# LayerNorm statistics without the square root on ScalarE, issued two tiles ahead, in a fused attention and spiking feed-forward kernel

## The chip, the cores and the metric

The kernel runs on the 8 cores of one Trainium2 chip. Each core takes one batch element (4096 tokens of 1024 channels) and runs the same program; nothing passes between the cores. The metric is the device time of the slowest core, in microseconds, for one execution.

## What is computed

```python
xn = layernorm(x)                     # (x - mean) / sqrt(var + 1e-5), per token, C = 1024
# attention in windows: qkv = xn @ w_qkv; windows of 4 tokens, every 2 tokens, 8 heads
dots = einsum('bnqhd,bnkhd->bnhqk', q, k) * scale
o = einsum('bnhqk,bnkhd->bnqhd', softmax(dots), v)
s = scatter_add(o @ w_out + b_out)    # every token lies in two windows
# feed-forward with a spiking neuron of 5 steps
h = square(relu(xn @ W_fc.T));  y = h @ W_proj.T
g = silu(sum_over_5_steps(spike) / 5)
out = x + s * g
```

The five steps of the neuron depend on `y` alone and are computed as five thresholds on it.

## The kernel before

The program has two phases. Phase A (up to about 1336 us) does the LayerNorm, the projections and the windowed attention, and leaves xn transposed and the attention result `st` in DRAM. Phase C does the feed-forward on blocks of 256 tokens and writes the output. The change touches phase A only.

Phase A works on tiles of 128 tokens (32 of them) in groups of four; the loop over `i` (0 to 9) has four steps `j` each, so a step is numbered k = 4i + j. In step k three things are interleaved, each for another part of the sequence:

- LayerNorm of tile `tln` = k (for i up to 7): `ln_load` brings x into one of two `xt` buffers (the buffer is tln % 2), `ln_stats` computes mean and 1/sqrt, `ln_apply` writes the normalised tile in bf16 to one of two `xnb` buffers, `xn_transpose` turns it with eight TensorE transposes into a `pp` bank and copies it to `xnT` (on VectorE for even tiles, on ScalarE for odd ones).
- Projection of the group before (for i from 1 to 8): each step has two chunks, `qk_super` (four heads, 32 matmuls and four evictions on ScalarE) in steps j = 0 and 1, `v_tile` (16 matmuls, two evictions) in steps j = 2 and 3. The banks `pp0` and `pp1` serve all chunks and transposes in turn.
- Attention of tile t = k - 8 (for i from 2): `scores(t, g)` for two halves g of the heads, `softmax_merge(t, g)` (four exponentials on ScalarE, L496 and L501, then two reduces, a reciprocal and eight small merges on VectorE), `wt_and_o(t - 1, g)`, and `st_tile(t - 1)`, the output projection of the tile before, whose result VectorE adds the bias to (L604, L606) and SP stores (`st_sc<-stt`).

Each engine has one queue that it works off in the order in which the code is written; nothing is reordered. In a step of before the code is in this order: `ln_apply(k)`, `ln_load(k + 2)`, `scores` and `softmax_merge` of g = 0, first chunk, `scores` and `softmax_merge` of g = 1, `wt_and_o`, second chunk, `st_tile`, `xn_transpose(k)`, `ln_stats(k + 1)`.

`Walk2.op` records the instructions and works out the semaphore waits from names of buffers; where a buffer's last user has no semaphore yet, it takes the last instruction recorded so far on that engine, so a wait can be for a later instruction than the one that used the buffer. The reads of `xt` are: a sum on VectorE (L316), then a sum of squares by a Square activation with an accumulator on ScalarE (L318), which waits for L316 since both write `astat`. From these VectorE makes mean, variance (L321 to L325), ScalarE takes the square root (L328), VectorE the reciprocal and the bias (L331, L333), and ScalarE applies them (L342).

At the start SP issues eleven small loads of constants (L276 to L281), all of which every engine's first instruction waits for, POOL's first load of `w_qkv` too.

Of the kernel before, what the change touches and what calls it, by code (L numbers as in the profile page):

```python
# [7 lines left out]
F32 = mybir.dt.float32  # L8
# [144 lines left out]
def build_program(L=4096):  # L153
# [23 lines left out]
    rfL = np.zeros((128, 1), np.float32); rfL[126:128] = -0.5  # L177
    zer_h = nc.inline_tensor(np.zeros((128, 1), np.float32), "c_zero")
    eps_h = nc.inline_tensor(np.full((128, 1), 1e-5, np.float32), "c_eps")
    rz0_h = nc.inline_tensor(rz0, "c_rz0")  # L180
    rzL_h = nc.inline_tensor(rzL, "c_rzL")
    rf0_h = nc.inline_tensor(rf0, "c_rf0")
# [4 lines left out]
    def sb(name, shape, dtype, off):  # L187
        A[name] = nc.alloc_sbuf_tensor_at(name, shape, dtype, offset=SB_BASE + off)
        return A[name]

    sb("eye", [128, 128], BF16, 0)
    sb("ones1", [1, 128], F32, 256)
    sb("mA", [128, 132], BF16, 768)
# [82 lines left out]
    for name, hdl in (("eye", eye_h), ("ones1", ones_h), ("mA", mA_h),  # L276
                      ("mB", mB_h), ("rz0", rz0_h), ("rzL", rzL_h),
                      ("rf0", rf0_h), ("rfL", rfL_h), ("zero", zer_h),
                      ("eps", eps_h)):
        dma("sp", A[name][:], hdl.ap(), "smc", (), ("consts", "bout"))  # L280
    dma("sp", A["bout"][:], bout_d, "smc", (), ("consts", "bout"))  # L281
    for _e in ENGS:
# [23 lines left out]
    def ln_load(t):  # L306
        p = t % 2
        dma("sp", A["xt"][:, C * p: C * (p + 1)], x_d[128 * t:128 * (t + 1), :],
            "sx" + str(p), (), (f"xt{p}",), ckpt=True)

    def ln_stats(t):
        p = t % 2
        xt = A["xt"][:, C * p: C * (p + 1)]
        xn = A["xnb"][:, C * p: C * (p + 1)]
        st = A["astat"][:, 8 * p: 8 * p + 8]
        w.op("ve", lambda E, o=st, i=xt: E.tensor_reduce(o[:, 0:1], i, AX.X, ALU.add),  # L316
             reads=(f"xt{p}",), writes=(f"astat{p}",))
        w.op("ae", lambda E, i=xt, s=st, d=xn: E.activation(d, i, AF.Square,  # L318
                                                            accum_out=s[:, 1:2]),
             reads=(f"xt{p}",), writes=(f"astat{p}", f"xnb{p}"))  # L320
        w.op("ve", lambda E, s=st: E.tensor_scalar(s[:, 2:3], s[:, 0:1], inv_c, None, ALU.mult),  # L321
             reads=(f"astat{p}",), writes=(f"astat{p}",))
        w.op("ve", lambda E, s=st: E.tensor_tensor(s[:, 3:4], s[:, 2:3], s[:, 2:3], ALU.mult),
             reads=(f"astat{p}",), writes=(f"astat{p}",))
        w.op("ve", lambda E, s=st: E.scalar_tensor_tensor(  # L325
            s[:, 4:5], s[:, 1:2], inv_c, s[:, 3:4], ALU.mult, ALU.subtract),
             reads=(f"astat{p}",), writes=(f"astat{p}",))
        w.op("ae", lambda E, s=st: E.activation(s[:, 5:6], s[:, 4:5], AF.Sqrt,  # L328
                                                bias=A["eps"][:, 0:1]),
             reads=(f"astat{p}", "consts"), writes=(f"astat{p}",))  # L330
        w.op("ve", lambda E, s=st: E.reciprocal(s[:, 6:7], s[:, 5:6]),  # L331
             reads=(f"astat{p}",), writes=(f"astat{p}",))
        w.op("ve", lambda E, s=st: E.scalar_tensor_tensor(  # L333
            s[:, 7:8], s[:, 2:3], -1.0, s[:, 6:7], ALU.mult, ALU.mult),
             reads=(f"astat{p}",), writes=(f"astat{p}",))

    def ln_apply(t):
        p = t % 2
        xt = A["xt"][:, C * p: C * (p + 1)]
        xn = A["xnb"][:, C * p: C * (p + 1)]  # L340
        st = A["astat"][:, 8 * p: 8 * p + 8]
        w.op("ae", lambda E, i=xt, s=st, d=xn: E.activation(  # L342
            d, i, AF.Identity, scale=s[:, 6:7], bias=s[:, 7:8]),
             reads=(f"xt{p}", f"astat{p}"), writes=(f"xnb{p}",))
# [287 lines left out]
    for j in range(2):  # L632
        ln_load(j)
    ln_stats(0)
    for i in range(NS + 2):
        p, qcons = i - 1, i - 2
        if i == NS:
# [6 lines left out]
                  if 0 <= p < NS else [])  # L644
        for j in range(4):
            tln = 4 * i + j
            if i < NS:
                ln_apply(tln)
                if tln + 2 < NT:
                    ln_load(tln + 2)  # L650
            t = 4 * qcons + j
            if qcons >= 0:
                scores(t, 0)
                softmax_merge(t, 0)
            for ch in chunks[2 * j: 2 * j + 1]:
                (qk_super(*ch[1:]) if ch[0] == "qk" else v_tile(ch[1]))
            if qcons >= 0:
                scores(t, 1)
                softmax_merge(t, 1)
                if t >= 1:  # L660
                    wt_and_o(t - 1, 0)
                    wt_and_o(t - 1, 1)
            for ch in chunks[2 * j + 1: 2 * j + 2]:
                (qk_super(*ch[1:]) if ch[0] == "qk" else v_tile(ch[1]))
            if qcons >= 0 and t >= 1:
                st_tile(t - 1)
            if i < NS:
                xn_transpose(tln)
                if tln + 1 < NT:
                    ln_stats(tln + 1)  # L670
        if i >= 2 and (i - 2) % 2 == 0 and (i - 2) // 2 < 3:
            xnsc_block((i - 2) // 2)
        if i == NS:
# [170 lines left out]
```

How the kernel before makes its waits and increments, by code:

```python
        def body(E):  # L802
            watermark = {}
            for rec in w.prog[eng_name]:
                for s, v in sorted(rec["waits"].items()):
                    if v > 0 and watermark.get(s, -1) < v:
                        E.wait_ge(sems[s], v)
                        watermark[s] = v
                instr = rec["fn"](E)
                if rec["inc"] is not None:
                    instr = instr.then_inc(sems[rec["inc"][0]], rec["inc"][1])
                if rec.get("inc2") is not None:
                    instr.then_inc(sems[rec["inc2"][0]], rec["inc2"][1])
```

## Time and profile before

| what | us |
|---|---|
| median of the runs (2357.06 to 2360.82) | 2358.94 |
| the profiled execution | 2354.82 |
| span of its slowest core (core 0) | 2353.3 |
| spans of the other cores | 2342.7 to 2351.8 |

The profile is of core 0. The median of the runs is 4.1 us above the profiled execution. Over the span PE is busy 1706.7 us (73%), ScalarE (ACT) 764.5 us, VectorE (DVE) 721.1 us. In a timeline row the columns are start, duration, engine, line, operation, and in brackets how long the engine sat idle before it and what released it. SPq is the queue of SP, which issues DMAs.

### The profile page before, as it was taken

Reading aid. Unit: us, or ns where it says so; the run is one execution under the profiler, and the core shown is the slowest. Engines: PE = TensorE matmul, PEld = TensorE weight load, DVE = VectorE, ACT = ScalarE, POOL = GpSimd, SP = SyncE. Lnnn points to the kernel's source line nnn. Section 1 sums busy time; section 2 is a strip of 40 time slices with the busy share of each in tenths; the row PEclk is TensorE's granted clock in tenths of the full one; section 3 lists DMA queues with packets and bytes.
Section 4 is the critical chain, followed back from the end, with each engine's and each line's share of the span. In section 5 each row is a group of like instructions: output and inputs, shape, how many; then the busy total and the mean of one; then the engine's idle time right before and its main releaser. Section 6 shows DMA issues by size and latency. Waiting matters only on the chain.

```text
span 2353.3 us, 29180 instructions; the slowest of 8 cores (2342.7 to 2353.3 us)
## 1 busy us (share of the span) xinstructions
PE 1706.7 (73%) x10595; PEld 998.8 (42%) x10708; DVE 721.1 (31%) x1561; ACT 764.5 (32%) x1702; POOL 29.9 (1%) x60
## 2 busy tenths in 40 slices
PE   1366575666565665656675519999999999999997
PEld 0123232323233333323332206666666666666664
DVE  1013423333333324232334411222333333333222
ACT  2143323232323232322211004444444444444442
POOL 0000000000000000000000000000000000000000
PEclk9998687787777786876886659999999999999998
DMA  4510010030100200100205431111111111112110
GB/s 100 101 42 14 23 54 23 19 58 14 51 26 27 47 23 21 54 14 14 36 10 105 92 79 39 55 54 55 55 54 55 54 55 55 55 55 63 55 61 21
DMA packets 55585, 111.05 MB, mean 47 GB/s; under 512 B 7314, under 2 KB 23699, under 8 KB 54420
## 3 DMA queue, kind: packets, MB, share of 16 engines
q1 hardware_dynamic: 47380, 84.02, 10.8%
q0 software_dynamic: 8064, 25.17, 6.7%
q8 instruction: 87, 1.43, 0.3%
q14 instruction: 54, 0.44, 0.1%
HBM read 100.77 MB, written 33.55 MB: 57 GB/s over the span
## 4 chain that ended last, share of the span: by engine, by line
PE 50%; ACT 20%; DVE 13%; issue 11%; DMA 5%; DVEq 1%; ACTq 0%; another core or an unknown queue 0%; SPq 0%; POOLq 0%
PE pp L387 9%; PE psB L742 9%; PE psA L742 9%; ACT hrl L724 7%; PE pO L598 5%; PE pp L406 4%; ACT hsb L727 4%; PE pO L721 3%; DMA wq<-w_qkv 3%; PE pO L565 2%; PE pO L581 2%; DVE wb L527 2%; PE pp L721 2%; ACT expB L501 2%; DVE wb L523 2%
## 5 line engine op out<-in xcount | busy, mean ns | idle before, releaser
L387 PE MATMUL pp<-xnT,wq 128*128 128x512 bf16 (+1 forms) x994 | 273.6, 435 | 148.6 <-ACT kr L391 54.7
L721 PE MATMUL pO<-xnTc,wfcT 128*128 128x256 bf16 x2688 | 326.1, 273 | 6.7 <-ACT hrl L724 6.7
L721 PEld LDWEIGHTS pO<-xnTc,wfcT 128*128 128x128 bf16 x2688 | 262.5, 98 | 42.3 <-issue 11.4
L387 PEld LDWEIGHTS pp<-xnT,wq 128*128 128x128 bf16 x1024 | 107.1, 109 | 306.2 <-issue 228.6
L742 PE MATMUL psA<-wprT,hsb 128*128 128x512 bf16 x992 | 219.3, 379 | 24.1 <-ACT hsb L727 23.3
L724 ACT ACTIVATE hrl<-pp 128x256 bf16<-128x256 f32 x176 | 66.1, 376 | 514.8 <-PE pp L721 514.8
L727 ACT ACTIVATE hsb<-hrl 128x256 bf16<-128x256 bf16 x512 | 213.6, 417 | 50.2 <-ACT hrl L724 3.7
L742 PE MATMUL psB<-wprT,hsb 128*128 128x512 bf16 x1008 | 222.8, 379 | 0.8
L721 PE MATMUL pp<-xnTc,wfcT 128*128 128x256 bf16 x1408 | 183.3, 273 | 45.4 <-DMA xi<-x 45.4
L749 DVE TENSOR_SCALAR acc<-psA 128x512 f32<-128x512 f32 x32 | 22.0, 686 | 570.7 <-PE psA L742 570.7
L565 PE MATMUL pO<-wtm,vr 128*128 128x128 bf16 x256 | 71.5, 279 | 164.3 <-DVE wte L551 164.3
L721 PEld LDWEIGHTS pp<-xnTc,wfcT 128*128 128x128 bf16 x1408 | 138.0, 98 | 65.5 <-issue 46.1
L742 PEld LDWEIGHTS psA<-wprT,hsb 128*128 128x128 bf16 x1024 | 100.0, 98 | 140.0 <-issue 23.9
L406 PE MATMUL pp<-wq,xnT 128*128 128x512 bf16 x482 | 140.4, 450 | 22.4 <-ACT xnb L318 7.2
L742 PEld LDWEIGHTS psB<-wprT,hsb 128*128 128x128 bf16 x1024 | 100.1, 98 | 120.9
L598 PE MATMUL pO<-wo,osb 128*128 128x512 bf16 x507 | 125.1, 403 | 6.5 <-DVE osb L585 6.2
L724 ACT ACTIVATE hrl<-pO 128x256 bf16<-128x256 f32 x336 | 126.1, 375 | 1.1 <-PE pO L721 1.1
L604 DVE TENSOR_TENSOR stt<-pO,b 128x512 bf16<-128x512 f32 x32 | 22.1, 692 | 313.9 <-PE pO L598 313.9
L410 ACT ACTIVATE vr<-pp 128x512 bf16<-128x512 f32 x64 | 37.0, 610 | 239.6 <-PE pp L406 239.6
L475 PE MATMUL psA<-mA,eye 128*128 128x132 bf16 x256 | 59.9, 234 | 73.6 <-ACT expB L501 73.6
L565 PEld LDWEIGHTS pO<-wtm,vr 128*128 128x128 bf16 x256 | 26.2, 102 | 201.4 <-issue 179.2
L506 DVE TENSOR_REDUCE rsb<-expA 128x4 f32<-128x528 bf16 x64 | 45.0, 703 | 191.0 <-ACT expB L501 191.0
(79 smaller groups left out, 1749.1 us busy)
## 6 DMA issues: line engine op xcount, KB each, us to landing
xt<-x SPq DMA_DIRECT2D x32, 512.0 KB, 3.5
xi<-x SPq DMA_DIRECT2D x32, 512.0 KB, 3.5
out<-ot SPq DMA_DIRECT2D x32, 512.0 KB, 2.7
st_sc<-stt SPq DMA_DIRECT2D x32, 256.0 KB, 2.0
xnT_sc<-xnT SPq DMA_DIRECT2D x32, 256.0 KB, 2.5
wprT<-w_projT POOLq DMA_DIRECT2D x32, 256.0 KB, 3.8
wfcT<-w_fcT POOLq DMA_DIRECT2D x8, 1024.0 KB, 10.1
xnTc<-xnT_sc SPq DMA_DIRECT2D x128, 64.0 KB, 2.0
```

Source lines behind the costliest of these rows:

```text
L387: E.matmul(d, lt, r, start=st_, stop=sp_)),
L406: E.matmul(d, lt, r, start=st_, stop=sp_)),
L475: E.matmul(d, A["eye"][:], r, start=st_, stop=sp_)),
L501: E.activation(o.rearrange("p (h j) -> p h j", h=2), p_[:].rearrange("p (h j) -> p h j", h=2)[:, :, 0:132], AF.Exp, scale=SCALE),
L523: E.tensor_scalar(o, i, r, None, ALU.mult),
L527: E.scalar_tensor_tensor(o, i, r, o, ALU.mult, ALU.add),
L565: E.matmul(d, lt, r, start=st_, stop=sp_)),
L598: E.matmul(d, lt, r, start=st_, stop=sp_)),
L721: E.matmul(d, lt, r, start=s, stop=p_)),
L724: w.op("ae", lambda E, d=hr, i=dst: E.activation(d, i, AF.Relu), reads=(bk,), writes=(f"hrl{fc % 2}",))
L727: E.activation(d, i, AF.Square),
L742: E.matmul(d, lt, r, start=s, stop=p_)),
```

## The change

The square root and the reciprocal leave: ScalarE's L328 and VectorE's L331 are replaced by a bit-shift start value and two Newton steps on VectorE (eps is now added there), 15 small instructions of 128x1 where there were five. The statistics of tile k + 2 are issued at the end of step k, instead of those of tile k + 1; `ln_apply(k)` and `ln_load(k + 2)` move from the start of step k to its end, just ahead of `xn_transpose(k)`. Two constants are added to the loads at the start. Line numbers below L174 grow by 2 to 21.

```diff
+    c15_h = nc.inline_tensor(np.full((128, 1), 1.5, np.float32), "c_c15")
+    cmag_h = nc.inline_tensor(np.full((128, 1), 0x5F3759DF, np.int32), "c_cmag")
...
-                      ("eps", eps_h)):
+                      ("eps", eps_h), ("c15", c15_h), ("cmag", cmag_h)):
...
+        w.op("ve", lambda E, s=st: E.tensor_scalar(s[:, 3:4], s[:, 3:4], -1e-5, None, ALU.add),
+             reads=(f"astat{p}",), writes=(f"astat{p}",))
         w.op("ve", lambda E, s=st: E.scalar_tensor_tensor(
             s[:, 4:5], s[:, 1:2], inv_c, s[:, 3:4], ALU.mult, ALU.subtract),
              reads=(f"astat{p}",), writes=(f"astat{p}",))
-        w.op("ae", lambda E, s=st: E.activation(s[:, 5:6], s[:, 4:5], AF.Sqrt,
-                                                bias=A["eps"][:, 0:1]),
+        w.op("ve", lambda E, s=st: E.tensor_scalar(
+            s[:, 5:6].bitcast(i32), s[:, 4:5].bitcast(i32), 1, None,
+            ALU.logical_shift_right),
+             reads=(f"astat{p}",), writes=(f"astat{p}",))
+        w.op("ve", lambda E, s=st: E.scalar_tensor_tensor(
+            s[:, 5:6].bitcast(i32), s[:, 5:6].bitcast(i32), -1,
+            A["cmag"][:, 0:1], ALU.mult, ALU.add),
              reads=(f"astat{p}", "consts"), writes=(f"astat{p}",))
-        w.op("ve", lambda E, s=st: E.reciprocal(s[:, 6:7], s[:, 5:6]),
-             reads=(f"astat{p}",), writes=(f"astat{p}",))
+        for fin in (False, True):
+            ydst = st[:, 6:7] if fin else st[:, 5:6]
+            w.op("ve", lambda E, s=st: E.tensor_tensor(s[:, 1:2], s[:, 5:6], s[:, 5:6], ALU.mult),
+                 reads=(f"astat{p}",), writes=(f"astat{p}",))
+            w.op("ve", lambda E, s=st: E.tensor_tensor(s[:, 1:2], s[:, 4:5], s[:, 1:2], ALU.mult),
+                 reads=(f"astat{p}",), writes=(f"astat{p}",))
+            w.op("ve", lambda E, s=st: E.scalar_tensor_tensor(
+                s[:, 3:4], s[:, 1:2], -0.5, A["c15"][:, 0:1], ALU.mult, ALU.add),
+                 reads=(f"astat{p}", "consts"), writes=(f"astat{p}",))
+            w.op("ve", lambda E, s=st, d=ydst: E.tensor_tensor(d, s[:, 5:6], s[:, 3:4], ALU.mult),
+                 reads=(f"astat{p}",), writes=(f"astat{p}",))
...
     ln_stats(0)
+    ln_stats(1)
...
             tln = 4 * i + j
-            if i < NS:
-                ln_apply(tln)
-                if tln + 2 < NT:
-                    ln_load(tln + 2)
...
             if i < NS:
+                ln_apply(tln)
+                if tln + 2 < NT:
+                    ln_load(tln + 2)
                 xn_transpose(tln)
-                if tln + 1 < NT:
-                    ln_stats(tln + 1)
+                if tln + 2 < NT:
+                    ln_stats(tln + 2)
```

The places in the queues that matter are at a boundary between two steps of the main part. First ScalarE, before, at the boundary behind a step j = 2 of which the tile is even (VectorE copies the transposes). The first row is the evictions of the last chunk, the last ones the exponentials and the evictions of the next step (j = 3).

```order
L410 ACTIVATE vr<-pp 128x512 [waits sem_pe] x2
L318 ACTIVATE xnb,astat<-xt 128x1024 [waits sem_sx1,sem_ve]
L328 ACTIVATE astat<-astat,eps 128x1 [waits sem_ve]
L342 ACTIVATE xnb<-xt,astat 128x1024 [waits sem_ve]
L496 ACTIVATE expA<-psA 128x264 [waits sem_pe]
L501 ACTIVATE expB<-psB 128x264
```

Now, at a boundary with an even tile (here behind a step j = 0, so that the evictions are those of `qr`), ScalarE has:

```order
L412 ACTIVATE qr<-pp 128x512 [waits sem_pe] x4
L363 ACTIVATE xnb<-xt,astat 128x1024
L322 ACTIVATE xnb,astat<-xt 128x1024 [waits sem_pe,sem_sx0,sem_ve]
L517 ACTIVATE expA<-psA 128x264 [waits sem_pe]
L522 ACTIVATE expB<-psB 128x264
```

The activation that applies the statistics moved from behind the sum of squares to ahead of it and waits for nothing new; L328 is gone; the sum of squares (L322) stands directly ahead of the exponentials.

Second SP's queue in the main part, before; `sem_sst` are the semaphores of the stores, `sem_sx` those of the loads, `sem_ae` ScalarE's and `sem_ve` VectorE's:

```order
L260 DMA st_sc<-stt 128x1024 [waits sem_sst0,sem_ve]
L260 DMA xt<-x 128x1024 [waits sem_ae,sem_sx1,sem_ve]
L260 DMA st_sc<-stt 128x1024 [waits sem_sst1,sem_ve]
L260 DMA xt<-x 128x1024 [waits sem_ae,sem_sx0,sem_ve]
```

and now:

```order
L264 DMA st_sc<-stt 128x1024 [waits sem_sst0,sem_ve]
L264 DMA xt<-x 128x1024 [waits sem_ae,sem_sx0]
L264 DMA st_sc<-stt 128x1024 [waits sem_sst1,sem_ve]
L264 DMA xt<-x 128x1024 [waits sem_ae,sem_sx1]
```

Stores and loads still alternate, but the load that follows a store is now that of the same boundary, two tiles ahead, and what it waits for on ScalarE is the activation that stands ahead of the transposes.

Third VectorE, now, at a boundary with an even tile, from the bias additions of `st_tile` to the first reduce of the next softmax:

```order
L625 TENSOR_TENSOR stt<-pO,b_56 128x512 [waits sem_pe,sem_sst1]
L627 TENSOR_TENSOR stt<-pO,b_56 128x512
L380 COPY xnT<-pp 128x8x128 [waits sem_pe]
L320 TENSOR_REDUCE astat<-xt 128x1 [waits sem_ae,sem_sx0]
L325 TENSOR_SCALAR astat<-astat 128x1 [waits sem_ae]
L327 TENSOR_TENSOR astat<-astat 128x1 [waits sem_ve]
L329 TENSOR_SCALAR astat<-astat 128x1 [waits sem_ve]
L331 SCALAR_TENSOR_TENSOR astat<-astat 128x1 [waits sem_ve]
L335 TENSOR_SCALAR astat<-astat 128x1 [waits sem_ve]
L339 SCALAR_TENSOR_TENSOR astat<-astat,cmag 128x1 [waits sem_ve]
```

Behind these come four instructions of a Newton step twice (L345, L347, L349, L352), L354, and then the first reduce of `softmax_merge`. The reduce L320 stands at the same place as L316 did; it reads a buffer whose load is now issued at this same boundary.

## Rows read from the trace of the kernel before

**Rows 1.** Busy time by stretch (engines, then PE clock, DMA share, GB/s): phase A's middle, phase C.
```profile
186.00:1110.00 924.00, 573.81 (x3161) 282.65 (x3204) 316.04 (x841) 268.02 (x472) 8.45 (x16) 0.75 0.11 30
1335.00:2353.30 1018.30, 913.45 (x6190) 610.07 (x6240) 291.21 (x415) 410.44 (x1061) 2.11 (x4) 0.96 0.17 54
```

**Rows 2.** What PE waited for from 186 to 1110 us: total, times, longest.
```profile
PE pO L565 <- DVE wte L551: 119.8, 46, 4.5
PE psA L475 <- ACT expB L501: 67.4, 12, 6.2
```

**Rows 3.** Timeline at an even boundary (steps j = 2 and 3), columns as described above.
```profile
909.87 0.32 SPq L260 DMA_DIRECT2D st_sc<-stt  x1
910.30 1.21 DVE L316 TENSOR_REDUCE astat<-xt 128x1 f32<-128x1024 f32 x1
912.86 0.15 DVE L321 TENSOR_SCALAR astat<-astat 128x1 f32<-128x1 f32 x1 [1.35 <-ACT xnb L318]
913.12 0.16 DVE L323 TENSOR_TENSOR astat<-astat 128x1 f32<-128x1 f32 x1
913.63 1.28 ACT L328 ACT_TABLE_LOAD   x1 [0.87 <-DVE astat L325]
917.11 1.28 ACT L496 ACT_TABLE_LOAD   x1
918.40 0.39 ACT L496 ACTIVATE expA<-psA 128x264 bf16<-128x264 f32 x1
919.74 0.70 DVE L506 TENSOR_REDUCE rsb<-expA 128x4 f32<-128x528 bf16 x1 [3.99 <-ACT expB L501]
923.72 0.39 ACT L496 ACTIVATE expA<-psA 128x264 bf16<-128x264 f32 x1 [3.10 <-DVE wb L523]
```

**Rows 4.** Timeline at an odd boundary (steps j = 1 and 2), the same rows of it.
```profile
873.76 1.21 DVE L316 TENSOR_REDUCE astat<-xt 128x1 f32<-128x1024 f32 x1
873.93 0.32 SPq L260 DMA_DIRECT2D st_sc<-stt  x1
883.20 0.70 DVE L506 TENSOR_REDUCE rsb<-expA 128x4 f32<-128x528 bf16 x1 [3.99 <-ACT expB L501]
```

**Rows 5.** Timeline of steps j = 0 and 1: PE behind their starts, and the second exponentials.
```profile
789.30 3.40 PE L387 MATMUL pp<-xnT,wq 128*128 128x512 bf16 x15 [2.83 <-ACT xnb L318]
796.95 3.60 PE L387 MATMUL pp<-xnT,wq 128*128 128x512 bf16 x9 [4.26 <-ACT qr L391]
803.32 0.39 ACT L496 ACTIVATE expA<-psA 128x264 bf16<-128x264 f32 x1 [0.38 <-PE psB L480]
840.54 5.89 PE L387 MATMUL pp<-xnT,wq 128*128 128x512 bf16 x16 [7.22 <-ACT kr L391]
847.50 0.39 ACT L496 ACTIVATE expA<-psA 128x264 bf16<-128x264 f32 x1 [0.38 <-PE psB L480]
```

**Rows 6.** The loads of x, by tile: time from issue to landing.
```profile
DMA to landing us min/median/max: 3.3/3.5/7.8
```

**Rows 7.** Timeline of the start: constants, first loads of x, first projection.
```profile
19.02 0.32 SPq L260 DMA_DIRECT2D eps<-c_eps  x1
21.04 0.29 SPq L260 DMA_DIRECT2D bout<-b_out  x1
22.65 0.81 SPq L260 DMA_DIRECT2D xt<-x  x2
91.72 5.71 PE L387 MATMUL pp<-xnT,wq 128*128 128x512 bf16 x13 [35.57 <-DMA wq<-w_qkv]
```

**Rows 8.** ScalarE's table loads, by line.
```profile
L496 ACT ACT_TABLE_LOAD x24 | 30.8, 1283 | 0.4
L328 ACT ACT_TABLE_LOAD x23 | 29.5, 1283 | 20.1 <-DVE astat L325 20.1
```

**Rows 9.** Timeline of the second group of steps (i = 1): PE behind ScalarE.
```profile
142.30 3.61 PE L406 MATMUL pp<-wq,xnT 128*128 128x512 bf16 x16 [2.13 <-ACT vr L410]
170.31 3.61 PE L387 MATMUL pp<-xnT,wq 128*128 128x512 bf16 x16 [2.97 <-ACT qr L391]
```

More of the change, by code:

```diff
@@ L189, in sb @@
         return A[name]
+    sb("c15", [128, 1], F32, -64)
+    sb("cmag", [128, 1], mybir.dt.int32, -32)
     sb("eye", [128, 128], BF16, 0)
@@ L327, in ln_stats @@
              reads=(f"astat{p}",), writes=(f"astat{p}",))
-        w.op("ae", lambda E, s=st: E.activation(s[:, 5:6], s[:, 4:5], AF.Sqrt,
-                                                bias=A["eps"][:, 0:1]),
-             reads=(f"astat{p}", "consts"), writes=(f"astat{p}",))
-        w.op("ve", lambda E, s=st: E.reciprocal(s[:, 6:7], s[:, 5:6]),
-             reads=(f"astat{p}",), writes=(f"astat{p}",))
+        i32 = mybir.dt.int32
+        w.op("ve", lambda E, s=st: E.tensor_scalar(
[5 more added lines that the diff above has]
+            A["cmag"][:, 0:1], ALU.mult, ALU.add),
+             reads=(f"astat{p}", "consts"), writes=(f"astat{p}",))
+        for fin in (False, True):
[9 more added lines that the diff above has]
+                 reads=(f"astat{p}",), writes=(f"astat{p}",))
         w.op("ve", lambda E, s=st: E.scalar_tensor_tensor(
```

## The prediction

> **What bounds the kernel now.** I read the busy times by stretch first, to find where the change can matter. In phase C PE is busy 913 of 1018 us and none of the changed code runs there [rows 1]. In the middle of phase A, from 186 to 1110 us, PE is busy 574 of 924 us, VectorE 316, ScalarE 268, at a granted clock of 0.75: no engine is full, so what counts is the chain of waits from engine to engine. The view of what PE waited for names two large ones there: 119.8 us in 46 waits for VectorE's `wte` copy, which stands in VectorE's queue behind the softmax merge, and 67.4 us in 12 waits for the exponentials [rows 2].
>
> Then I followed one boundary between two steps in the timeline [rows 3]. VectorE starts the sum of x (L316) at 910.30. Square, small statistics, a table load for the square root at 913.63, apply, and a table load back for Exp at 917.11 follow in one chain; the exponentials start at 918.40, which is 8.1 us behind the sum, and VectorE's merge of the first half at 919.74. The second exponentials wait for that merge until 923.72, and everything up to the end of the step hangs on them. So in steps j = 2 and 3 (short chunks) the end is set by when the **first merge starts on VectorE**. In steps j = 0 and 1 (32 matmuls in a chunk) the second exponentials wait last for PE's scores (847.50, 0.38 idle behind PE), and PE waited 7.22 us for the evictions, which stand behind the exponentials on ScalarE [rows 5]. There the end is set by when **ScalarE is free for exponentials and evictions**. These two go different ways under this change.
>
> **The change at a boundary.** Gone from ScalarE's chain: two table loads of 1.28 us, the square root, and the apply of 1.24 us, which now runs beneath `st_tile`'s 16 matmuls. VectorE's small instructions are 15 instead of 5, and they stand in a row ahead of the first merge, where the last of them was followed by a wait of 3.99 us for the exponentials. The sum and the Square now read a buffer whose load is issued at this boundary. SP issues it behind the store of `stt`: the store at 909.87 [rows 3], the load 0.48 us behind it (two DMAs in a row take 0.81 us with 0.33 for the second [rows 7]), landing 3.5 us later [rows 6], and 0.1 for the engine to start. So the sum starts at 913.95 instead of 910.30.
>
> - Even boundary: the Square chain ends as before 2.46 us behind the sum's start (the first small instruction is at +2.56 [rows 3]), so exponentials start at 916.4 instead of 918.40, **2.0 us earlier**. The small instructions start at 916.5 and are 0.265 us apart (912.86, 913.12), the 15th ends at 920.3, the merge starts there instead of at 919.74: **0.6 us later**.
> - Odd boundary: before, the sum started at 873.76, just ahead of the store at 873.93, since ScalarE copies the transposes [rows 4]. Now the load goes at 874.41, the sum starts at 878.0, exponentials at 880.5, and the merge at 878.0 + 6.4 = 884.4 instead of 883.20: **1.2 us later**.
>
> The new integer instructions (shift, multiply-add) have no row. The nearest are the 128x1 ones of 0.15 to 0.16 us, which I take; if each took 0.1 us more the merge would start 0.2 us later, and below the 0.15 I see no room. For the load the lower end is 3.3 and the upper 7.8 us [rows 6], the latter beside the weight loads; I take the median, since the store ahead of it is half its size.
>
> **By kind of boundary** (statistics stand at 23 boundaries of the middle part now, into steps k = 8 to 30, where 24 had them):
>
> - Into j = 2 (odd), 6 times 1.2 = +7.2. Into j = 3 (even), 5 times 0.6 = +3.0. VectorE's chain ends last in both.
> - Into k = 31 the statistics are gone: the merge can start once the scores and exponentials are done, at about 911.4 on the scale of rows 3 instead of 919.74, -8.3.
> - Into j = 1 (even), 6 times: evictions 2.0 us earlier and PE too. PE's idle of 7.22 us, after which 16 matmuls took 5.89 us [rows 5] against 3.61 us in other places [rows 9], is split in two, since PE's second head now waits for the sum to end (its bank's release is marked there). Slow matmuls then lie partly inside the wait. I get -3.1 each, which is also where the merge becomes the last one (it ends 0.4 us later than before, some 3.4 us ahead of the old second exponentials). -18.6.
> - Into j = 0 (odd), 6 times: PE's first head already waited 2.83 us, to 789.30, for the Square, because the copy of the group's last tile is marked as ready only there [rows 5]. The Square now ends with the load: PE starts at 793.6, after 7 us idle instead of 2.83, so its first eight matmuls are slow (3.4 us, not 1.9). Head 2 ends at 799.2 and its eviction at 799.8, so the third head starts at 799.95 instead of 796.95, but then at full speed (3.6 us, not 5.3): second exponentials at 804.6 instead of 803.32. 5 times 1.3 = +6.5. Into k = 8, which had no slow matmuls before (3.61 behind a wait of 2.97 [rows 9]), +4.0.
> - In i = 1 there is no attention work to hide the apply, the load or the Square behind. Behind j = 0: apply and load move the transposes by 1.2 us, but the sqrt and apply behind the Square are gone: +0.7. Behind j = 1 (odd): PE resumes at 142.30 [rows 9]; the apply adds 1.2 us and the wait for the load, less the square root and apply behind the Square, 2.3; slow once, 1.5: +5.0. Behind j = 2: +1.1. Together +6.8.
> - Start: constants are 2.0 us apart on SP, and all wait for the last [rows 7]. POOL's weight loads start behind them, and PE's first projection at 91.72 waits for those (35.57 us idle), so two more constants cost +4.0. In i = 0 the longer steps lie inside that wait of 35 us: nothing. If that cover were gone, they would cost some 3.5 us each.
>
> Sum: 4.0 + 6.8 + 4.0 + 6.5 - 18.6 + 7.2 + 3.0 - 8.3 = **+4.6 us** against the profiled execution of 2354.8: 2359.4. The median of the runs shown stands 4.1 us above that execution, so I forecast **2363**. Phase C moves as a whole.
>
> **Rivals.**
>
> A. The table loads' price comes back. 23 + 24 of them at 1.283 us [rows 8]: all but one would be 59 us, and 2359 - 59 = 2300. It needs the load of x to be covered: without the 3.65 and 4.25 us that the sum starts later, all 23 boundaries would gain about 3.5 us more than in my sum, -80, to 2283. For it: the load needs only the apply, which is done beneath `st_tile`'s matmuls, ahead of the store. Against it: in SP's queue it stands behind the store. Take 2290. The Trainium skill (ScalarE: Activation LUTs, What ACT_TABLE_LOAD costs) says that a switch costs about 2.66 us, of which 1.38 is a drain behind the load; by that 46 switches would be 122 us, and the time about 2237. The rows here show the load at 917.11 and the exponential 1.29 us later [rows 3], so no such drain; the trace does not agree.
>
> B. The load lands later than 3.5 us. It now goes out with the store ahead of it, at three boundaries with eight stores of `xnT` behind it, and eight cores do so at once. Every microsecond more falls on 23 boundaries plus 3 in i = 1 and on VectorE, ScalarE and PE alike. From 5.3 us on (26 times 1.8 = 47) it is slower by 2%; at 6.0 us it would be 2363 + 65 = 2428. Against it: the median of 32 is 3.5 us, with the lowest at 3.3, so few of them are late.
>
> C. PE's clock. If each of the 26 boundaries costs one stretch of slow matmuls more on PE's path (1.7 us, 5.3 against 3.6), that is +44 less what I counted (about 12): 2395. For it: PE is at 0.75 here and idles in longer single pieces at odd boundaries. Against it: at even boundaries the idle is split.
>
> D. In steps j = 0 and 1 the gain is larger (the evictions are freed by 2.0 us and no head is slow): -2.0 or -1.4 for the evictions and -1.7 for the slow stretch, mean -3.4 at each of 12, -41, where my sum has -18.6 + 6.5 + 4.0 = -8. That is 33 less: 2330.
>
> **How the numbers follow.** A measurement of this kernel can tell about 2% from no change, so 2312 and 2410 are the bounds. My forecast with errors of a few tenths per boundary (2345 to 2385): 0.60. C and smaller forms of B (2385 to 2410): 0.15. D and smaller forms of A (2312 to 2345): 0.13. A in full: 0.04. B in full: 0.08. Range 2332 to 2402, which leaves out A and B in full and the ends of C and D, about 2 in 10. Faster 0.04, same 0.88, slower 0.08.
>
> **What would show it.** Right: table loads down from 47 at these two lines to one; at an even boundary the sum starts about 4.1 us behind the store of `stt` and waits for the load of x, where it waited for nothing; the exponentials start 6.5 us behind the store instead of 8.5; VectorE goes from the last small instruction into the merge without idling; first projection 4 us later. Wrong: a sum that starts right behind the store (A), landings of x above 5 us (B), a granted clock in the middle clearly under 0.75 (C), or VectorE idle ahead of the merge, which would mean that the small instructions are not last.

## The result, and the profile after

The changed kernel takes 2376.5 us (median), against 2358.9 us before; the ratio is 1.0078 with a 95% interval of 1.0067 to 1.009. In some executions, of any version, the cores of one half of the chip or of both run at a lower clock, and the times in this text leave these out. The change is slower by 0.8%, which is clear of no change but inside the 2% that the chances speak of. Forecast were 2363 us and a loss of 4.6; the loss is 17.7. The profiled execution took 2376.53 us, on its slowest core (core 2) with a span of 2374.8 us. Against the profiled execution of before (2354.82) the loss is 21.7 us, and the mean over the eight cores' spans rose by 21.2 us (2346.8 to 2368.0), so the loss is not one of a single core.

The table loads are gone as meant. These two, outside the steps, are all that are left; the 47 of [rows 8] are gone to the last one:

```profile
L300 ACT ACT_TABLE_LOAD x1 | 1.3, 1283 | 29.4 <-PE pp L297 29.4
L783 ACT ACT_TABLE_LOAD x1 | 1.3, 1283 | 0.0
```

The busy times by stretch answer to [rows 1]; the stretches are shifted because phase A has become longer. The first row is of before, for a stretch that is not shown ahead of the prediction.

```profile
91.70:186.00 94.30, 68.38 (x327) 29.73 (x334) 17.00 (x50) 34.53 (x59) 3.69 (x7) 0.96 0.21 43
```

```profile
96.00:190.00 94.00, 65.48 (x261) 26.22 (x260) 18.91 (x76) 27.45 (x44) 3.70 (x7) 0.80 0.21 42
190.00:1130.00 940.00, 602.94 (x3275) 288.68 (x3273) 354.19 (x1069) 204.24 (x412) 8.45 (x16) 0.76 0.11 30
1355.00:2374.00 1019.00, 918.87 (x6240) 609.81 (x6240) 291.82 (x416) 412.17 (x1061) 2.11 (x4) 0.96 0.17 54
```

Phase C is the same (1019 us, PE 919). In the middle PE's granted clock is nearly what it was (0.76 on core 2, before 0.75 on core 0; from the second merge of step 8 to the first of step 30 it is 0.75 on core 0, before 0.76), ScalarE is 64 us less busy, VectorE 38 us more, in a stretch that has grown from 924 to 940 us. In the first row of after, the steps of i = 1, the clock is 0.80, where the row of before has 0.96.

What PE waited for in the middle (total, times, longest) answers to [rows 2]:

```profile
PE pO L586 <- DVE wte L572: 119.9, 46, 4.6
PE psB L561 <- ACT expB L522: 75.7, 23, 6.4
PE pp L427 <- ACT xnb L322: 35.8, 6, 6.5
PE pp L408 <- ACT xnb L322: 35.1, 5, 7.3
PE pp L408 <- DVE astat L320: 24.6, 6, 5.2
PE pp L427 <- DVE astat L320: 20.4, 5, 4.6
```

Before, behind the two rows of [rows 2], the list went on with these:

```profile
PE psB L540 <- ACT expB L501: 59.1, 23, 3.7
PE pp L387 <- ACT kr L391: 47.9, 12, 7.2
PE pp L387 <- ACT qr L391: 23.8, 10, 4.3
```

The 119.8 us for the `wte` copy are untouched. The wait for the exponentials ahead of the second scores (67.4 us) is gone, and those for the evictions of `kr` and `qr` fell from 71.7 us to 19.9. In their place came 116 us for L320 and L322, the sum and the Square of x (before, 22), and the second wait for exponentials grew from 59.1 to 75.7. So PE's waits did not become shorter in sum; they moved. The sum and the Square do not take long; they wait for the load. The timeline of an even boundary shows it (core 2, into a step j = 1; [rows 3] is an even boundary of before, into j = 3):

```profile
856.13 0.32 SPq L264 DMA_DIRECT2D st_sc<-stt  x1
856.60 0.33 SPq L264 DMA_DIRECT2D xt<-x  x1
861.49 1.22 DVE L320 TENSOR_REDUCE astat<-xt 128x1 f32<-128x1024 f32 x1 [4.84 <-DMA xt<-x]
862.80 1.06 ACT L322 ACTIVATE xnb<-xt 128x1024 bf16<-128x1024 f32 x1 [9.85 <-DVE astat L320]
862.85 3.26 PE L408 MATMUL pp<-xnT,wq 128*128 128x512 bf16 x8 [5.17 <-DVE astat L320]
863.86 0.37 ACT L517 ACTIVATE expA<-psA 128x264 bf16<-128x264 f32 x1
864.05 0.15 DVE L325 TENSOR_SCALAR astat<-astat 128x1 f32<-128x1 f32 x1 [1.35 <-ACT xnb L322]
864.31 0.16 DVE L327 TENSOR_TENSOR astat<-astat 128x1 f32<-128x1 f32 x1
867.76 0.16 DVE L354 SCALAR_TENSOR_TENSOR astat<-astat 128x1 f32<-128x1 f32 x1
867.86 0.70 DVE L527 TENSOR_REDUCE rsb<-expA 128x4 f32<-128x528 bf16 x1
871.84 0.39 ACT L517 ACTIVATE expA<-psA 128x264 bf16<-128x264 f32 x1 [0.58 <-DVE wb L544]
```

The store goes out, the load 0.47 us behind it, and VectorE sits idle for 4.84 us until it lands. The exponentials start 7.7 us behind the store instead of 8.5. The fifteen small instructions follow each other 0.265 us apart, and the merge (L527) starts 0.1 us behind the start of the last without idling, 11.7 us behind the store where it was 9.9.

To see where time is lost I cut each step into three parts by the starts of VectorE's rows: from the first merge (L506, now L527) to the second, from there to the second bias addition (L606, now L627), and from there to the next step's first merge, which is the boundary. Means in us of the three parts over steps 12 to 29:

| steps | before, core 0 | after, core 0 | after, core 2 | change, mean of the eight cores |
|---|---|---|---|---|
| j = 0 | 8.75, 24.58, 10.64 | 8.67, 25.35, 11.23 | 8.32, 25.18, 11.95 | -0.21, +0.97, +0.89 |
| j = 1 | 9.17, 24.59, 10.04 | 6.56, 24.63, 11.42 | 5.89, 25.19, 12.07 | -2.92, +0.57, +1.60 |
| j = 2 | 5.49, 20.42, 10.63 | 5.52, 20.70, 11.21 | 5.52, 20.17, 11.75 | +0.03, +0.03, +0.73 |
| j = 3 | 5.65, 20.88, 10.04 | 5.49, 20.78, 11.22 | 5.49, 20.27, 11.48 | -0.16, -0.29, +1.24 |

The boundary in a row is the one behind that step. Four steps add up to 160.9 us before, and to 162.8 (core 0) and 163.3 us (core 2) after; the mean of the eight cores rose by 2.5 us.

### The profile page after: what moved, and what is told of

The parts are those of the page before. It is cut to its first block, busy times and chain, and to the rows that moved or that the text cites. A ratio compares the mean times of both kernels' runs of the same rounds, so it can differ in the third digit from the quotient of the medians.

```text
span 2374.8 us, 29820 instructions; the slowest of 8 cores (2362.6 to 2374.8 us)
## 1 busy us (share of the span) xinstructions
PE 1742.5 (73%) x10708; PEld 1001.5 (42%) x10708; DVE 773.4 (33%) x1881; ACT 693.9 (29%) x1623; POOL 29.9 (1%) x60
## 4 chain that ended last, share of the span: by engine, by line
PE 51%; ACT 15%; DVE 14%; DMA 10%; issue 9%; DVEq 1%; ACTq 0%; SPq 0%; POOLq 0%
PE pp L408 10%; PE psA L763 9%; PE psB L763 9%; ACT hrl L745 7%; PE pO L619 5%; DMA xt<-x 4%; PE pp L427 4%; ACT hsb L748 4%; PE pO L742 3%; DMA wq<-w_qkv 3%; PE pO L586 2%; DVE wb L548 2%; PE pO L602 2%; PE pp L742 2%; DVE wb L544 2%
## 5 line engine op out<-in xcount | busy, mean ns | idle before, releaser
L408 PE MATMUL pp<-xnT,wq 128*128 128x512 bf16 (+1 forms) x1024 | 286.6, 441 | 126.2 <-ACT xnb L322 38.8
L763 PE MATMUL psA<-wprT,hsb 128*128 128x512 bf16 x1024 | 223.6, 379 | 19.9 <-ACT hsb L748 19.9
L427 PE MATMUL pp<-wq,xnT 128*128 128x512 bf16 x512 | 166.6, 492 | 68.5 <-ACT xnb L322 38.6
L763 PEld LDWEIGHTS psA<-wprT,hsb 128*128 128x128 bf16 x1024 | 99.8, 98 | 140.2 <-issue 24.1
L427 PEld LDWEIGHTS pp<-wq,xnT 128*128 128x128 bf16 x512 | 57.7, 119 | 161.0 <-issue 134.5
L561 PE MATMUL psB<-eye,wb 128*128 128x128 bf16 x256 | 34.3, 279 | 99.6 <-ACT expB L522 99.6
```

Of the source, the lines that this page charges most:

```text
L408: E.matmul(d, lt, r, start=st_, stop=sp_)),
L427: E.matmul(d, lt, r, start=st_, stop=sp_)),
L763: E.matmul(d, lt, r, start=s, stop=p_)),
```

## The experiments

All results are ratios to the kernel before, run beside them on the same chip. In the code cuts `...` marks lines left out.

### The math alone

The Newton steps and the constants, in the order of before (the cut is against the changed kernel; `ln_apply` and `ln_load` also leave the end of the step):

```diff
-    ln_stats(1)
...
+            if i < NS:
+                ln_apply(tln)
+                if tln + 2 < NT:
+                    ln_load(tln + 2)
             t = 4 * qcons + j
...
-                if tln + 2 < NT:
-                    ln_stats(tln + 2)
+                if tln + 1 < NT:
+                    ln_stats(tln + 1)
```

> The Newton steps and the two constants in the order of before; load, apply and statistics stay where they were. Theory (only the chain from the sum of x to the exponentials counts, and table loads are one link of it): the chain keeps the apply and gets 15 small instructions of 0.265 us in place of two table loads, the square root and five small ones, so the exponentials start 7.8 us behind the sum instead of 8.1. 24 boundaries times -0.3, plus 3 us for the constants at the start: about 2354 (2348 to 2362), no change. Rival (the price of 46 table loads comes back, 59 us, once nothing else is moved): 2303.

Measured: 1.0044 (1.0031 to 1.0058), 2367.6 us. The table loads' 59 us do not come back; the rival is out. But it is 10 us slower, outside the range of the theory (2348 to 2362). At an odd boundary of the middle part:

```profile
889.01 1.21 DVE L320 TENSOR_REDUCE astat<-xt 128x1 f32<-128x1024 f32 x1
895.51 1.24 ACT L363 ACTIVATE xnb<-xt,astat 128x1024 bf16<-128x1024 f32 x1 [4.05 <-DVE astat L354]
896.65 0.37 ACT L517 ACTIVATE expA<-psA 128x264 bf16<-128x264 f32 x1
897.96 0.70 DVE L527 TENSOR_REDUCE rsb<-expA 128x4 f32<-128x528 bf16 x1 [2.55 <-ACT expB L522]
```

The exponentials start 7.64 us behind the sum and the merge 8.95, where before [rows 4] the merge came 9.44 behind it: 0.5 us less, a little more than expected. The loss lies ahead of the middle: the first merge of step 8 starts at 183.8 us (core 0) instead of 169.3. Of these 14.5 us, 5.1 are the start (PE's first projection at 96.86 instead of 91.72). In i = 1 no exponential had run yet, so the square root needed no table load there. From the first small instruction to the activation that applies the statistics it took 1.7 us before and 4.3 now (both core 0, behind j = 0), and PE waits that much longer. First before, then now:

```profile
120.38 5.29 PE L387 MATMUL pp<-xnT,wq 128*128 128x510 bf16 x16 [3.37 <-ACT kr L391]
154.68 5.30 PE L406 MATMUL pp<-wq,xnT 128*128 128x512 bf16 x16 [3.37 <-ACT vr L410]
```

```profile
127.04 5.71 PE L408 MATMUL pp<-xnT,wq 128*128 128x510 bf16 x16 [5.97 <-ACT kr L412]
```

The granted clock over the 77 us ahead of step 8 fell with it, from 0.96 to 0.89 on every core. I had counted no loss there. In the middle the boundaries are 0.4 us shorter, but the part behind the second merge is 0.9 and 0.8 us longer in j = 0 and 1 and 0.6 in j = 2 (means of the eight cores).

### The order alone

The square root and reciprocal of before in the new order (against the kernel before):

```diff
-            if i < NS:
-                ln_apply(tln)
-                if tln + 2 < NT:
-                    ln_load(tln + 2)
             t = 4 * qcons + j
...
             if i < NS:
+                ln_apply(tln)
+                if tln + 2 < NT:
+                    ln_load(tln + 2)
                 xn_transpose(tln)
-                if tln + 1 < NT:
-                    ln_stats(tln + 1)
+                if tln + 2 < NT:
+                    ln_stats(tln + 2)
```

> The order of the change with the square root and the reciprocal of before, no constants added. Theory: the table loads still lie behind the Square, so against the change the exponentials start 3.7 us later and the merge about 1.2 us later at each boundary. 11 boundaries into j = 2 and 3 times 1.2, 12 into j = 0 and 1 times 2 to 3, less 3 us at the start: 2376 + 40 = about 2416 (2400 to 2430). Rival (the table loads are hidden beneath the wait for the load, so the math is worth nothing and the order alone costs what the change costs): 2374.

Measured: 1.0224 (1.0193 to 1.0255), 2409.3 us, in the range of the theory (2400 to 2430); the rival is out. ScalarE at a boundary:

```profile
885.56 1.06 ACT L318 ACTIVATE xnb<-xt 128x1024 bf16<-128x1024 f32 x1 [8.71 <-DVE astat L316]
887.58 1.28 ACT L328 ACT_TABLE_LOAD   x1 [0.87 <-DVE astat L325]
889.19 1.28 ACT L496 ACT_TABLE_LOAD   x1
890.49 0.39 ACT L496 ACTIVATE expA<-psA 128x264 bf16<-128x264 f32 x1
```

Both table loads lie between the Square and the exponentials. So the order alone costs 2.2% and the math alone 0.4%; together they cost 0.8%, because in the new order the math takes out a chain that the order has put behind the load. The boundaries are 12.55 to 12.72 us, against 11.2 to 12.1 under the change.

### The load ahead of the store

Against the changed kernel:

```diff
+            if i < NS:
+                ln_apply(tln)
+                if tln + 2 < NT:
+                    ln_load(tln + 2)
             if qcons >= 0 and t >= 1:
                 st_tile(t - 1)
             if i < NS:
-                ln_apply(tln)
-                if tln + 2 < NT:
-                    ln_load(tln + 2)
                 xn_transpose(tln)
```

> The change, with apply and load of x written ahead of st_tile, so that SP issues the load of x ahead of the store of stt. Theory (the added wait is the load of x, issued too late): the load goes out at the end of the apply, about 3 us before the store, and the sum starts about 3.3 us earlier at each of 26 boundaries; into j = 1 some of it is lost. About -70 us against the change: 2305 (2290 to 2320), faster than before by 2%. Rival (VectorE's 15 small instructions and PE's clock set the step, the load only fills their time): less than 25 us, above 2350.

Measured: 0.9748 (0.9726 to 0.9771), some 2298 us, in the range of the theory. Nothing is computed differently from the change; SP only issues the load some 3 us earlier. The boundaries fall to 7.8 to 8.5 us, and the four steps take 148.7 us instead of 163.3. This shows where the loss in the middle comes from: with the load issued 3 us sooner the time is 78 us less, more than the 59 us of the table loads. The load is still not covered; VectorE starts the sum 0.9 us behind the store (mean), where before it was 0.1 us and under the change 4.1 to 4.5. In i = 1 nothing is gained: step 8 is reached at 185.5 us on core 0, under the change at 185.2.

### The statistics beneath the second chunk

```diff
-    ln_stats(1)
...
+            if i < NS and tln + 1 < NT:
+                ln_stats(tln + 1)
             for ch in chunks[2 * j + 1: 2 * j + 2]:
...
                 xn_transpose(tln)
-                if tln + 2 < NT:
-                    ln_stats(tln + 2)
```

to the edit above.

> The same math, with the statistics of tile k + 1 (whose load is a step old) written ahead of the second chunk of step k, and apply and load ahead of st_tile. ScalarE is idle for 14 us there and VectorE for 8 to 13 us. Theory (in steps of the middle part only what stands between the bias additions and the exponentials counts): nothing of the statistics is left at the boundary, the merge starts 1.6 us behind the bias additions instead of 10 to 11. 24 times -8.5 = -204, with 3 us of constants and a little in i = 1: 2155 (2130 to 2190). Rival (PE becomes the bound once the waits go, in steps j = 0 and 1 above all): half of that, 2255.

Measured: 0.9279 (0.9254 to 0.9304), 2188 us; 7.2% faster than before, at the upper end of the theory's range.

```profile
703.22 1.21 DVE L320 TENSOR_REDUCE astat<-xt 128x1 f32<-128x1024 f32 x1
704.52 1.06 ACT L322 ACTIVATE xnb<-xt 128x1024 bf16<-128x1024 f32 x1 [12.84 <-DVE astat L320]
709.46 0.16 DVE L354 SCALAR_TENSOR_TENSOR astat<-astat 128x1 f32<-128x1 f32 x1
713.72 0.33 SPq L264 DMA_DIRECT2D xt<-x  x1
715.40 0.69 DVE L625 TENSOR_TENSOR stt<-pO,b 128x512 bf16<-128x512 f32 x1 [5.78 <-PE pO L619]
716.01 0.68 DVE L627 TENSOR_TENSOR stt<-pO,b 128x512 bf16<-128x512 f32 x1
716.69 0.39 ACT L517 ACTIVATE expA<-psA 128x264 bf16<-128x264 f32 x1 [3.10 <-PE psB L501]
718.02 0.70 DVE L527 TENSOR_REDUCE rsb<-expA 128x4 f32<-128x528 bf16 x1 [0.74 <-ACT expB L522]
```

Sum, Square and small instructions are through at 709.6, while PE does the second chunk; VectorE then idles 5.78 us until the bias addition. The exponentials wait for nothing but the scores, and the merge starts 2.0 us behind the second bias addition. The boundary has shrunk to 2.0 to 2.2 us. Some of it is given back where PE is next: in steps j = 0 and 1 the second merge comes 9.4 and 10.2 us behind the first, the exponentials there now waiting last for PE's scores. PE's granted clock in the middle is 0.82, before 0.75 [rows 1].

```profile
190.00:950.00 760.00, 555.76 (x3313) 272.78 (x3312) 350.92 (x1064) 204.27 (x404) 9.49 (x18) 0.82 0.13 38
```

### One Newton step instead of two

```diff
-        for fin in (False, True):
+        for fin in (True,):
```

> The change with one Newton step instead of two, so 11 small instructions instead of 15 (the result is less exact; nothing else is left out). Theory (in steps j = 2 and 3, and by now j = 1, the first merge on VectorE ends last, and the small instructions stand ahead of it): four times 0.265 = 1.06 us less at 11 boundaries into j = 2 and 3, some 0.8 at 6 into j = 1, nothing into j = 0: -16 us, 2376 to 2360. Rival (the step hangs on the load, the Square and ScalarE alone; VectorE has slack): 2376.

Measured: 1.0039 (1.0024 to 1.0054), 2364.7 us, so 9 to 12 us less than the change, where the theory had 16. Every boundary is shorter: 10.2 to 10.3 us on core 2, and by 1.1 us in the mean of the eight cores, which is the four instructions' 1.06 us. In j = 0 and j = 1 the second merge then comes later behind the first (9.74 us instead of 8.32, and 7.65 instead of 5.89, core 2), which gives it back; for j = 0 that was expected. So VectorE's small instructions are on the path in j = 2 and 3.

The same cut in the version with hidden statistics:

> e4_stats_hidden with one Newton step instead of two: the same four small instructions fewer as in e5_one_newton, which gained 12 us there. Theory (they cost only where they stand ahead of the merge; here they run beneath the second chunk): no change, 2185 (within 4 us). Rival (VectorE's total work counts too): -8 to -12, 2175.

Measured: 0.9285 (0.9262 to 0.9308), 2186.4 us, against 0.9279 with two steps: no change. The same four instructions are worth some 10 us in one place and nothing that can be measured in the other.

### Hidden statistics with the square root kept

The order of the version with hidden statistics, with the math of before and no constants added.

> The order of e4_stats_hidden with the square root and reciprocal of before, no constants added. Theory (a table load costs where it stands: the one for the square root is now beneath the second chunk, the one back for Exp is still ahead of the exponentials, behind their wait for the scores): 24 times 1.28 = +31, less 3 at the start: 2188 + 28 = 2216. Rival (the load back for Exp runs in ScalarE's idle time before the scores are done): 2185, the math is then worth nothing.

Measured: 0.9495 (0.9454 to 0.9536), 2228.5 us in the profiled execution, 45 us above that of the version with Newton steps, more than the 28 expected (one of its three executions took 2251.1 us, hence the wide interval; by the ratios it is 51). The rival is out. The load back for Exp (core 0):

```profile
746.42 1.28 ACT L496 ACT_TABLE_LOAD   x1 [3.08 <-PE psB L480]
747.71 0.39 ACT L496 ACTIVATE expA<-psA 128x264 bf16<-128x264 f32 x1
750.51 3.11 PE L387 MATMUL pp<-xnT,wq 128*128 128x512 bf16 x8 [2.44 <-DVE rsb L509]
754.46 5.27 PE L387 MATMUL pp<-xnT,wq 128*128 128x512 bf16 x16 [0.84 <-ACT kr L391]
```

ScalarE sat idle for 3.08 us for the scores and only then loaded the table: the load did not run in the idle time ahead of it. It is so at twelve of the 24 loads (2.1 to 3.3 us of idle time; cores 0 and 1); the others, but for one on core 1, follow directly behind other work and had no idle time to run in. The boundaries are 3.3 to 3.5 us instead of 2.0 to 2.2, 1.35 times 23 = 31. The other 14 us lie within the steps, above all in j = 1, where the second merge comes 12.55 us behind the first, against 10.21 (core 0); in the rows above PE waits 2.44 us and its 24 matmuls take 3.1 + 5.3 us. That the slow matmuls make up the rest is argued from these rows, not shown. So the math of the change is worth 45 us, once the order does not hide it behind a load.

### The constants alone

The two constants are loaded and never read:

```diff
-                      ("eps", eps_h)):
+                      ("eps", eps_h), ("c15", c15_h), ("cmag", cmag_h)):
```

> The kernel before with the two constants loaded and never read. Theory: two more loads of 1.4 to 2.0 us on SP ahead of everything, the weight loads start 3 us later and PE's first projection with them: +3 us (2 to 4), ratio 1.0013. Rival (the first projection waits for the last weight load, whose end is set by bandwidth that was shared with the loads of x): no change.

Only one execution is left; it took 2354.8 us, where those of before ran from 2352 to 2358, so there is no ratio. The spans of single cores can be compared: over 28 undisturbed ones of this kernel the mean is 2350.7 us, over 80 of before 2347.6, which makes 3.1 us, as expected. The trace shows the start:

```profile
96.02 6.29 PE L391 MATMUL pp<-xnT,wq 128*128 128x512 bf16 x15 [37.17 <-DMA wq<-w_qkv]
```

PE's first projection starts at 96.02 instead of 91.72 [rows 7], and the first merge of step 8 at 173.3 instead of 169.3 (both core 0). The 4 us are there at step 8, and some 3 of them are left at the end.

### Weights before the constants

The version with hidden statistics, with POOL's queue freed from the wait for the constants:

```diff
     for _e in ENGS:
+        if _e == "gp":
+            continue
         w.barrier_waits[_e] = {"smc": w.cnt["smc"]}
```

> e4_stats_hidden, with POOL's queue not waiting for the constants, so that the weight loads start at 1 us instead of 26. Theory (PE's first projection waits for the weights alone, 25 us of idle): it starts where the LayerNorm of tile 3 ends, or 25 us earlier, whichever is later: -20 us, 2188 to 2168. Rival (the loads of x then share the bandwidth and the LayerNorm of the first tiles is late): -5, 2183.

Measured: 0.9285 (0.9271 to 0.9299), the same as without it. A miss, and the rival too named the wrong thing in part:

```profile
1.56 0.66 POOL L264 DMA_DIRECT2D wq<-w_qkv  x1 [0.87 <-POOLq L156]
51.90 0.29 SPq L264 DMA_DIRECT2D bout<-b_out  x1
97.66 5.95 PE L410 MATMUL pp<-xnT,wq 128*128 128x512 bf16 x15 [1.48 <-DVE astat L354]
```

The weight loads start at 1.56 us, but beside them most of the small loads of constants go out 3.5 to 8 us apart; the last goes out at 51.9 us instead of 24.1. The LayerNorm of the first tiles starts that much later. PE's transposes at 95.18 waited 6.70 us for the activation that applies the statistics, and the first projection at 97.66 comes behind them instead of waiting for the weights.

### The first steps apart

The change from step 7 on, and the placement of the hidden statistics in the steps before:

```diff
-    ln_stats(1)
...
+            if i < 2:
+                ln_stats(tln + 1)
             for ch in chunks[2 * j + 1: 2 * j + 2]:
...
-                if tln + 2 < NT:
+                if 7 <= tln < NT - 2:
                     ln_stats(tln + 2)
```

> The change from step 7 on; in steps 0 to 6 (and once more in step 7) the statistics of tile k + 1 stand ahead of the second chunk, as in e4_stats_hidden, and none at the end of the step. Theory (some 13 us of the change's loss arise in i = 1, where nothing covers apply, load and Square, and PE's matmuls run slow behind those waits): the first merge of step 8 starts about 12 us earlier than under the change and all that follows with it: 2376 to 2364. Rival (an early gain there is lost again before the end of phase A, as the 4 us of the constants seem to be): above 2372.

Measured: 1.0048 (1.0035 to 1.006), 2364.7 us. The first merge of step 8 starts at 168.1 us (core 0; 171.2 on the slowest, core 5) instead of 185.2 and 185.1 under the change; the time is 7 to 12 us less. The middle part is the same as under the change to 0.1 us in every column of the table (core 0). Over the eight cores the mean span is 2355.4 us, under the change 2368.0 and before 2346.8. So i = 1 is about half of the change's loss (12.6 of 21.2 us in these means), and the middle the rest. On core 5 only 7 of the 14 us are left at the end of phase A; it is a core that loses 4 us in step 31, which most others do not, as core 0 does before and core 2 after.

## Why the prediction was right or wrong, point by point

The range held (2332 to 2402), and so did the side, but the sum was too small by 13 us between medians and by 17 between the profiled executions, to which its rows belong. Nothing cancelled: both stretches that were wrong were too small. What kept the time in the range is its width. Set against the trace (before on core 0, after on core 2, the slowest of each; last, the mean change of the eight cores):

| stretch | predicted | measured | mean of eight |
|---|---|---|---|
| to the second merge of step 8 (start, i = 1, into k = 8) | 4.0 + 6.8 + 4.0 = +14.8 | 176.34 to 194.67 = +18.3 | +18.0 |
| from there to the first merge of step 30 | -18.6 + 6.5 + 7.2 + 3.0 = -1.9 | 869.5 to 880.3 = +10.8 | +11.7 |
| step 30 to 31, where the statistics are gone | -8.3 | 37.1 to 28.1 = -9.0 | -8.7 |
| to the first merge of step 39 | 0 | +0.4 | +0.6 |
| from there to the end | 0 | +0.9 | -0.3 |

- **What bounds the kernel.** Right: the chain at the boundary, by the first merge in j = 2 and 3. The load ahead of the store and the hidden statistics shorten that chain and the time with it, and one Newton step less helps only where it stands ahead of the merge.
- **The price of the boundary** (0.6 us at an even one, 1.2 at an odd one). Right on core 0: the means rose by 0.6 behind j = 0 and 2 and by 1.4 and 1.2 behind j = 1 and 3. On the slowest core they rose by 1.1 to 2.0, in the mean of the eight by 0.9 and 0.7 at the even ones and by 1.6 and 1.2 at the odd ones. For the landing of the load I took 3.5 us and 0.1 for the engine. From the issue to the start of the sum it was 3.6 us on core 0 and 4.05 on core 2 (means of 21 boundaries), 3.75 over the eight cores. The median landing of all 32 is 3.5 us on cores 0 and 6, 3.6 to 3.7 on five others, and on core 2:

```profile
DMA to landing us min/median/max: 3.4/4.0/6.9
```

  This is rival B in small: some 10 us on core 2 and some 3 in the mean (an estimate, 23 times 0.45 and 0.15). It is not the main error: core 0, where the load landed as I took it, lost 7.9 us in the middle, and core 3, with a median of 3.6, lost 14.1. Which core lands its loads late, and which is the slowest, stays open; in other executions of the changed kernel the slowest was core 0, 1, 3, 4 or 5.
- **Into j = 1** (-3.1). This is the term that was most in error. The second merge comes 3.3 us sooner behind the first on core 2 (9.17 to 5.89), 2.6 on core 0 and 2.9 in the mean, for the -3.7 of my sum (3.1 and the 0.6 of the boundary). The mechanism is right: in the timeline above the second exponentials wait 0.58 us for the merge, no longer for PE. But the boundary ahead grew by more than 0.6 and the part behind the second merge by 0.6, so the whole step with its boundary gained only 1.5 us in the mean of the eight cores. Six times 1.6 are some 10 of the 13.6 us by which the middle was too small in that mean; into j = 0 (+2.0 for +1.3) and j = 2 (+1.7 for +1.2) are most of the rest.
- **Into j = 0** (+1.3). 8.75 to 8.32 and a boundary longer by 1.4 give +1.0: right so far. (My 5.3 us for the third head are the 5.30 of the 16 matmuls from 796.95; the row in [rows 5] shows nine of them.) Not foreseen: the middle part, which no edit touches, is 0.6 to 0.8 us longer in j = 0 (24.58 to 25.18 and 25.35), with its second chunk's 16 matmuls in 5.67 us at one place. The same work runs slower there. It does so with the math alone and with the order alone too (by 0.9 and 1.0 us in j = 0, means of the eight cores), so it needs neither the late load nor the small instructions; why in these steps and not in j = 2 and 3 is open.
- **i = 1** (+6.8) and into k = 8 (+4.0). Too small by 4.4 us with the start, which was 3.1 (91.72 to 94.80) instead of 4.0. I had counted one slow stretch of matmuls more in i = 1. PE in these steps, core 2:

```profile
124.49 5.51 PE L408 MATMUL pp<-xnT,wq 128*128 128x510 bf16 x16 [0.84 <-ACT kr L412]
151.38 5.72 PE L427 MATMUL pp<-wq,xnT 128*128 128x512 bf16 x16 [0.84 <-ACT vr L431]
167.93 5.98 PE L427 MATMUL pp<-wq,xnT 128*128 128x512 bf16 x16 [0.84 <-ACT vr L431]
182.07 5.74 PE L408 MATMUL pp<-xnT,wq 128*128 128x512 bf16 x16 [3.66 <-ACT xnb L322]
```

  Sixteen matmuls took 5.5 to 6.0 us at four places behind waits of 0.84 us (3.66 before the last), where PE had waited 2.8 to 3.3 us in the middle of the chunk. Before, two such places had 5.3 us (120.38 and 154.68, above) and the others 3.61 [rows 9]. The granted clock says the same, on every core: over the 77 us ahead of step 8 it was 0.96 on all eight before, and after it is 0.89 on core 1, which loses least (its first merge of step 8 at 176.8 us, 12 later), and 0.76 on core 4, which loses most (189.3, 24.5 later). So rival C came true in i = 1; in the middle the clock hardly moved. Taking the statistics out of the way there brings step 8 forward by 14 to 17 us on cores 0 and 5, and the clock of core 0 back to 0.91 (92 to 170 us of that run).
- **k = 31** (-8.3). -9.0.
- **Rival A** (the table loads come back). Out for this change: math alone, +0.4%. The condition that I gave for it, a covered load, was the right one: with the load ahead of the store the kernel is 2.5% faster than before (I had 2290, measured 2298). The Trainium skill (ScalarE: Activation LUTs, What ACT_TABLE_LOAD costs) adds a drain of about 1380 ns to each load of about 1283; no trace here shows one: the load takes 1283 ns, and the exponential starts 1.29 us behind the load's start, in the kernel before (917.11 to 918.40) and with hidden statistics (746.42 to 747.71).
- **Rival D** (a larger gain in j = 0 and 1). Out: into j = 1 the gain is 1.5 us, into j = 0 there is a loss of 2.0 (means of the eight cores), where D had a gain of 3.4 in each.
- **The signs.** The exponentials start 7.7 us behind the store, not 6.5; the sum starts 4.1 us behind it on core 0, as said, and 4.5 on core 2. VectorE goes into the merge without idling.

The expected gain, then, did not vanish: it was paid away. The math is worth 45 us where its place is free, and the order costs 2.2% by itself: it moved the load from a place where it had a whole step to one where the engines wait for it, as the load ahead of the store shows, and it took the cover from i = 1.

## What to carry to other kernels

When a computation is moved ahead, list the transfers that it reads and where their issue now stands in the issuing queue: a lookahead of two with two buffers leaves a load no time, and a store ahead of it in the queue costs it more. Ask first where the engines that must do the work are idle: the same statistics, one tile ahead and beneath the second chunk, made the kernel 7% faster. Four of the fifteen small instructions no longer mattered then, but the table load that still stood ahead of the exponentials did (45 us). An instruction count is worth nothing without its place: four small instructions were worth some 10 us ahead of the merge and nothing beneath a chunk.

## What the runs showed of the hardware

- The table load of ScalarE starts only when the wait of the activation that needs it is over, not in the idle time ahead: with hidden statistics and the square root kept, 2.1 to 3.3 us idle and then the load of 1.28 us, at twelve of 24 places.
- Small constant loads of SP's queue, at most 2.9 us apart by themselves, go out mostly 3.5 to 8 us apart beside POOL's 768 KB weight loads.
- The load of 512 KB lands in 3.5 us (median of 32) on cores 0 and 6 and in 4.0 on core 2 in the same execution.
- Integer shift and multiply-add of 128x1 on VectorE take 153 and 160 ns, as the float ones (154 and 160), and a row of fifteen such instructions on the same small tile runs at 0.265 us apiece.
- Longer waits of PE in i = 1 went with a lower granted clock on all eight cores: 0.96 before, 0.89 with the math alone, 0.76 to 0.89 under the change.
